# Attention weights loaded as F32 on the SP and ACT queues, mask tiles of twice the size, and deeper loads in the second half

## The reference

```python
x = x + 0.5 * ffn(layernorm(x))          # hidden 4096, inner 11008, int8 weights with scales
x = x + attn(layernorm(x))
x = x + 0.5 * ffn(layernorm(x))

def attn(data, mask, weight, bias):      # weight, mask: 4096 x 4096; mask is int32
    bm = mask.reshape(128, 32, 128, 32).sum(axis=(1, 3)) > 0
    wb = weight.reshape(128, 32, 128, 32) * bm[:, None, :, None]
    return einsum('bsk,nk->bsn', data, wb.reshape(4096, 4096)) + bias

def ffn(x, ...):
    hidden = silu(qlinear(x, w_gate, s_gate)) * qlinear(x, w_up, s_up)
    return qlinear(hidden, w_down, s_down)
```

## Time and profile before

| what | us |
|---|---|
| median of the 2 runs shown | 9921.1 (9498.07 and 10344.14) |
| the profiled execution, whole | 8834.6 |
| its span on the slowest core (core 4) | 8832.8 |
| spans of all cores in it | 8821.7 to 8832.8 |
| mean granted TensorE clock of its cores | 0.944 to 0.963 |

### The profile page before, as it was taken

How to read it: one execution, slowest core, us unless ns; L and a number is a source line. 1 busy time by engine, 2 the same in 40 slices (tenths; PEclk the granted TensorE clock), 3 DMA queues, 4 the chain that set the end, 5 groups by cost and what they waited for, 6 DMA issues and landing times.

```text
span 8832.8 us, 84484 instructions; the slowest of 8 cores (8821.7 to 8832.8 us)
## 1 busy us (share of the span) xinstructions
PE 8020.2 (91%) x35567; PEld 3595.1 (41%) x36280; DVE 1532.0 (17%) x2276; ACT 1263.1 (14%) x1500; POOL 635.9 (7%) x1204
## 2 busy tenths in 40 slices
PE   5399999999577999999975999999997899999998
PEld 1144444444223444444442444444433344444444
DVE  0211111111443111111112111111112211111111
ACT  0511010012121101101014100101132210010111
POOL 1000000000000000000000000000000000000000
PEclk9599999999788999999986999999998999999998
DMA  9133434444484444443431444444333344444343
GB/s 158 57 143 145 155 153 148 152 153 141 105 174 133 153 151 153 162 144 153 150 133 70 153 150 152 152 151 158 148 121 100 127 153 147 153 153 154 148 151 134
DMA packets 201976, 1256.71 MB, mean 142 GB/s; under 512 B 23169, under 2 KB 23298, under 8 KB 113410
## 3 DMA queue, kind: packets, MB, share of 16 engines
q0 software_dynamic: 172800, 1149.32, 38.1%
q10 hardware_dynamic: 18432, 67.12, 2.1%
q1 hardware_dynamic: 10370, 34.83, 1.3%
HBM read 726.88 MB, written 50.33 MB: 88 GB/s over the span
## 4 chain that ended last, share of the span: by engine, by line
PE 88%; DVE 4%; DMA 3%; ACT 3%; issue 2%; DVEq 0%; ACTq 0%; SPq 0%; POOL 0%; POOLq 0%
PE PB L580 27%; PE PB L495 27%; PE PB L501 27%; PE PB L692 4%; DMA MB16D<-mask 2%; DVE WTM L651 1%; DVE XN L440 1%; ACT L341 1%; DMA wtmc<-WTM 1%; PE PB L278 1%; PE PB L737 1%; DVE GS L433 1%; DVE XN L436 1%; ACT L761 0%; ACT L303 0%
## 5 line engine op out<-in xcount | busy, mean ns | idle before, releaser
L495 PE MATMUL PB<-XN,GBUF 128*128 128x512 bf16 x10784 | 2425.6, 380 | 97.3 <-DVE XN L440 85.7
L501 PE MATMUL PB<-XN,UBUF 128*128 128x512 bf16 x10788 | 2417.8, 379 | 11.6
L580 PE MATMUL PB<-H,DBUF 128*128 128x512 bf16 x10786 | 2384.5, 380 | 35.6 <-DVE H L539 23.7
L495 PEld LDWEIGHTS PB<-XN,GBUF 128*128 128x128 bf16 x11008 | 1078.9, 98 | 1394.7 <-issue 102.1
L580 PEld LDWEIGHTS PB<-H,DBUF 128*128 128x128 bf16 x11008 | 1073.6, 98 | 1343.3 <-issue 66.0
L501 PEld LDWEIGHTS PB<-XN,UBUF 128*128 128x128 bf16 x11008 | 1077.0, 98 | 1298.9
L525 ACT ACT_TABLE_LOAD x344 | 441.4, 1283 | 5808.0 <-DVE GS L517 5808.0
L692 PE MATMUL PB<-XN,WTM 128*128 128x512 bf16 x2006 | 500.4, 409 | 215.2 <-DVE WTM L651 152.7
L592 DVE SCALAR_TENSOR_TENSOR R<-PB,SDV,R 128x512 f32<-128x512 f32 x384 | 288.3, 751 | 2148.6 <-PE PB L580 2098.3
L532 DVE SCALAR_TENSOR_TENSOR US<-PB,SUV,RB 128x512 f32<-128x512 f32 x344 | 258.5, 752 | 2092.7 <-PE PB L501 2092.7
L517 DVE SCALAR_TENSOR_TENSOR GS<-PB,SGV,RB 128x512 f32<-128x512 f32 x344 | 258.3, 751 | 1866.5 <-PE PB L495 1866.5
(11 more groups left out here) (58 smaller groups left out, 1205.1 us busy)
## 6 DMA issues: line engine op xcount, KB each, us to landing
GBUF<-wg POOLq DMA_DIRECT2D x344, 1024.0 KB, 5.1
UBUF<-wu POOLq DMA_DIRECT2D x344, 1024.0 KB, 7.1
DBUF<-wd POOLq DMA_DIRECT2D x256, 928.0 KB, 4.7
DBUF<-wd POOLq DMA_DIRECT2D x128, 896.0 KB, 4.7
ABUF<-wa POOLq DMA_DIRECT2D x64, 512.0 KB, 9.0
wtmc<-WTM ACTq DMA_DIRECT2D x64, 512.0 KB, 6.4
XIN<-x SPq DMA_DIRECT2D x32, 512.0 KB, 3.7
out<-OUT ACTq DMA_DIRECT2D x32, 512.0 KB, 2.6
```

The source lines that it names most:

```text
L495: ins = t.matmul(PB[0 + 2 * par][:], GB[par][:, dk * 128:(dk + 1) * 128], XN[:, dk * TH:(dk + 1) * TH], start=(dk == 0), stop=(dk == NDK - 1))
L501: ins = t.matmul(PB[1 + 2 * par][:], UB[par][:, dk * 128:(dk + 1) * 128], XN[:, dk * TH:(dk + 1) * TH], start=(dk == 0), stop=(dk == NDK - 1))
L580: ins = t.matmul(PB[4 + bpar][:], DB[spar][:, ik * 128:(ik + 1) * 128], H[:, ik * TH:(ik + 1) * TH], start=(ik == 0), stop=(ik == nik - 1))
```

## The change

Three edits. (1) The mask is loaded in 32 pieces of 128 x 4096 instead of 64 of 128 x 2048; the four buffers grow to 8 KB a partition, and INDR moves to the place of BMEP. (2) In the first half's attention wa is loaded as F32, without a cast, into two buffers instead of three, by SP for even slots and by ACT for odd slots instead of by POOL; the load of slot sl waits for mask sl-2 instead of sl-3, and the first two wait for the end of gate and up only. (3) In the second half the loads of wtmc run four slots ahead instead of two, each of the four WTM buffers with a semaphore of its own.

```diff
-    MB16A = sb("MB16A", [128, 2048], BF16, 161504)
-    MB16B = sb("MB16B", [128, 2048], BF16, 165600)
-    MB16C = sb("MB16C", [128, 2048], BF16, 169696)
-    MB16D = sb("MB16D", [128, 2048], BF16, 173792)
-    INDR = sb("INDR", [128, 32 * 128], BF16, 177888)
+    MB16A = sb("MB16A", [128, 4096], BF16, 161504)
+    MB16B = sb("MB16B", [128, 4096], BF16, 169696)
+    MB16C = sb("MB16C", [128, 4096], BF16, 177888)
+    MB16D = sb("MB16D", [128, 4096], BF16, 186080)
+    INDR = sb("INDR", [128, 32 * 128], BF16, 144608)
-    ABUF0 = sb("ABUF0", [128, 16 * 128], BF16, 161504)
-    ABUF1 = sb("ABUF1", [128, 16 * 128], BF16, 165600)
-    ABUF2 = sb("ABUF2", [128, 16 * 128], BF16, 169696)
+    ABUF0 = sb("ABUF0", [128, 16 * 128], F32, 161504)
+    ABUF1 = sb("ABUF1", [128, 16 * 128], F32, 169696)
...
-        for rh in range(64):
-            rt, ch = rh // 2, rh % 2
-            par = rh % 4
+        for rt in range(32):
+            par = rt % 4
...
                 psem.inc(gp.dma_start(
-                    MB16[par][:],
-                    mask[rt * 128:(rt + 1) * 128, ch * 2048:(ch + 1) * 2048]), 16)
+                    MB16[par][:], mask[rt * 128:(rt + 1) * 128, :]), 16)
...
-                for c4 in range(4):
-                    c = ch * 4 + c4
+                for c in range(8):
                     ins = t.matmul(PALL[:, c * 512:(c + 1) * 512],
                                    INDR[:, rt * 128:(rt + 1) * 128],
-                                   MB16[par][:, c4 * 512:(c4 + 1) * 512],
+                                   MB16[par][:, c * 512:(c + 1) * 512],
                                    start=(rt == 0), stop=(rt == 31))
...
-                    par = sl % 3
+                    par = sl % 2
                     wp = sl % 4
-                    qsem = (sem_n[0], sem_n[1], sem_n[2])[par] if hf == 0 else \
-                        (sem_d[0] if sl % 2 == 0 else sem_a[1])
-                    qblk = block.gpsimd if hf == 0 else \
-                        (block.sync if sl % 2 == 0 else block.scalar)
+                    qsem = (sem_d[0] if sl % 2 == 0 else sem_a[1]) if hf == 0 else \
+                        (sem_d[0], sem_a[1], sem_d[1], sem_a[0])[sl % 4]
+                    qblk = (block.sync if sl % 2 == 0 else block.scalar) if hf == 0 \
+                        else (block.sync, block.scalar, block.sync,
+                              block.scalar)[sl % 4]
...
-                            if sl < 3:
-                                eng.wait_ge(sem_t.h, mk[("t_d", hf, 1, 93 + par)])
+                            if sl < 2:
+                                eng.wait_ge(sem_t.h, t_gu1)
                             else:
-                                eng.wait_ge(sem_v.h, mk[("v_msk", hf, sl - 3)])
+                                eng.wait_ge(sem_v.h, mk[("v_msk", hf, sl - 2)])
...
-                            if sl < 2:
+                            if sl < 4:
                                 eng.wait_ge(sem_t.h, t_gu1)
                                 eng.wait_ge(sem_c[sl % 2].h, mk[("a_wtm", 0, 62 + sl % 2)])
                             else:
-                                eng.wait_ge(sem_t.h, mk[("t_am", hf, sl - 2)])
+                                eng.wait_ge(sem_t.h, mk[("t_am", hf, sl - 4)])
```

More of the change, by code:

```diff
@@ L115, in build_nc @@
     MB16 = [MB16A, MB16B, MB16C, MB16D]
-    AB = [ABUF0, ABUF1, ABUF2]
+    AB = [ABUF0, ABUF1]
     WTM = [WTM0, WTM1, WTM2, WTM3]
@@ L153, in build_nc, with pdma, pmm @@
         psems = (sem_g[0], sem_g[1], sem_n[0], sem_n[1])
-        for rh in range(64):
-            rt, ch = rh // 2, rh % 2
-            par = rh % 4
+        for rt in range(32):
+            par = rt % 4
             psem = psems[par]
-            def pdma(gp, rh=rh, rt=rt, ch=ch, par=par, psem=psem):
-                if rh < 4:
+            def pdma(gp, rt=rt, par=par, psem=psem):
+                if rt < 4:
                     gp.wait_ge(sem_d[0].h, d_init)
                 else:
-                    gp.wait_ge(sem_t.h, tmark_prep[rh - 4])
+                    gp.wait_ge(sem_t.h, tmark_prep[rt - 4])
                 psem.inc(gp.dma_start(
-                    MB16[par][:],
-                    mask[rt * 128:(rt + 1) * 128, ch * 2048:(ch + 1) * 2048]), 16)
+                    MB16[par][:], mask[rt * 128:(rt + 1) * 128, :]), 16)
             block.gpsimd(pdma)
             dneed = psem.n
-            def pmm(t, rh=rh, rt=rt, ch=ch, par=par, dneed=dneed, psem=psem):
+            def pmm(t, rt=rt, par=par, dneed=dneed, psem=psem):
                 t.wait_ge(psem.h, dneed)
                 ins = None
-                for c4 in range(4):
-                    c = ch * 4 + c4
+                for c in range(8):
                     ins = t.matmul(PALL[:, c * 512:(c + 1) * 512],
                                    INDR[:, rt * 128:(rt + 1) * 128],
-                                   MB16[par][:, c4 * 512:(c4 + 1) * 512],
+                                   MB16[par][:, c * 512:(c + 1) * 512],
                                    start=(rt == 0), stop=(rt == 31))
                 sem_t.inc(ins)
-                tmark_prep[rh] = sem_t.n
+                tmark_prep[rt] = sem_t.n
             block.tensor(pmm)
```

## The result

The changed kernel is slower by 3.5%: against the runs of the kernel before in the same comparison the ratio is 1.0349, 95% interval 1.0323 to 1.0375. The median of its 11 runs is 9597.62 us (9119.97 to 10674.91), that of ten runs of before 9331.72 us (8830.55 to 10344.14). So taken, the changed kernel takes 9120 to 9154 us and before 8829 to 8837. Spans of single cores go from 9090 to 9160 us with the change, the middle one 9113, and from 8816 to 8834 before, the middle one 8824 or 8825 in each of the three later comparisons.

What follows compares the result with a forecast made beforehand. Feed-forward TensorE lines led the chain; the mask stage ran at its transfers' pace and no engine was full in the first attention. 8834.6 + 304 (odd loads) + 2 (F32 masks) - 5 (second attention) = 9136 us, range 8965 to 9250.

Steps and rivals of the forecast that it cites:

- L: First attention: landing time of the odd wa load, forecast 9.5 us with colliding transfers, from 5.3 alone to 11.1.
- Order of ACT's stream: First attention: the odd load stands behind the even slot's write-back on ACT, so cannot leave before the even mask is done.
- The 16 matmuls B: First attention: TensorE's second 16 matmuls of a block, forecast 5.5 us, between 3.5 and 6.8.
- Block: First attention: one output block takes 21.7 us against 12.2, times 32 giving +304 us.
- Even loads and two buffers at no cost: First attention: even loads on SP with two buffers instead of three stay hidden, no cost.
- F32 source: First attention's mask multiplications: F32 instead of bf16 source adds 8 ns each, +2 us in all.
- Mask stage: Mask loads, 32 of 2 MB instead of 64 of 1 MB: same bytes, 0 us, with bounds of -11 and +1.9 us.
- Second attention: Second half: wtmc loads four slots ahead remove TensorE's waits, -5 us, with 0 and -6 as bounds.
- No collision: Rival, first attention: odd load waits its turn but is served as if alone, L 5.3; 9001 us, chance 0.18.
- Heavier collision: Rival, first attention: eight cores read and write at once and the PE stays slow; 9232 us, chance 0.11.
- The load gets past the wait: Rival, first attention: odd loads leave a block ahead, block stays at 12.2 us; 8832 us, chance 0.06.
- Mask stage bound per packet: Rival, mask stage: half the packets take half of 206 us, -103 us, total 9033; chance 0.03.

Runs made afterwards that it cites:

- the loads' change alone: Kernel before with edit (2) only: F32 loads, two buffers, SP and ACT, in the changed kernel's order; 9143.34 us, 1.035.
- the attempt to better the kernel: Kernel before with the next block's loads, masks and write-backs put ahead of L705, in both halves, bf16 cast by POOL; 8940.23 us, 1.2% more than before.
- the cast version: Kernel before with the next block's masks ahead of the residual in the first half only, bf16 cast by POOL; 8768.0 and 8772.6 us, ratio 0.9931.

## Why the prediction was right or wrong

**What it missed.** The stated time, 9136 us, and its range, 8965 to 9250, do not hold the median of the runs, 9597.62. The term of the sum that failed is its base, 8834.6 us: "I forecast on the profiled execution's footing". The median of the kernel before in the same comparison is 9331.72 us, 497 us above that base, and on this base the same sum, +304 + 2 - 5, gives 9633 us, 35 us from the measured median. The two runs shown stood 7.5% and 17% above the profiled execution and the prediction said so, yet its range ended at 9250, below the lower of them, 9498. Nothing in the change or the rows could tell how many of the runs would lie near the profile; with two runs shown, both far above it, either a range that reached up to them (9136 x 9921 / 8835 = 10259) or a ratio was called for.

**What it got.** The mechanism was right. On its own footing the sum was 3.4%, and 3.5% was measured by the slowest cores, 3.3% by the middle ones. That it comes so near is in part luck: L differs by 2 us from core to core, 64 us over 32 blocks, and 9.5 happens to lie inside. Its steps, with core 2 of the profile after:

- *Order of ACT's stream:* right, and shown twice, by moving the load ahead (loss gone) and by adding the lateness alone to the kernel before (about three quarters of it, by four cores).
- *Issue of the odd load:* 2.96 us after the masks begin; measured 3.05 (2707.67 to 2710.72).
- *Landing L:* 9.5 forecast. DVE goes on 9.41 us after the issue in the block shown; the median over the stage is 10.1 us on core 2, 10.6 on core 3, and 8.6 on cores 4 to 6. That L differs by 2 us between cores of one execution was not foreseen. It makes most of the 60 us between the spans of core 4 and core 2: DVE waits 302.2 us for the loads on core 4 and 343.0 on core 2, 41 us more, and 180.7 and 197.7 us for the matmuls ahead of L702, 17 us more.
- *Second mask to TensorE:* 2.85 forecast, 2.65 measured.
- *The 16 matmuls B:* 5.5 forecast; 6.49 in the block shown (2722.78 to 2729.27), 5.14 in the one before it (2701.62 to 2706.76). Over the 32 blocks DVE waits 197.7 us for TensorE ahead of L702, 6.18 a block, of which 0.39 lies outside these matmuls in the block shown (6.88 - 6.49): B is 5.8 us on average, and by the same working 5.3 on core 4. The forecast, a mean of two blocks, lies between.
- *Block:* 21.7 forecast, 22.5 measured on core 2 (721 us / 32); of the difference 0.7 us is L and 0.3 B. Stage: +304 forecast, +330 on core 2. The whole came 318 us above the profile of before on that core, and 258 on core 4.
- *Even loads and two buffers at no cost:* right for the buffers (8839 us with two). No wait for the even load is seen, but it makes 4 of the 10.1 us of the odd load's landing on core 2; holding it back brought about 80 us. The prediction had this collision as part of L.
- *F32 source:* +2 us forecast, L648 takes 684 ns against 685: nothing. The double rate on 16-bit data of the Trainium skill, VectorE: DVE Perf Modes (The perf-mode tier table), was rightly not charged: 685 ns with bf16 is no double rate beside 684 with F32.
- *Mask stage:* 0 forecast; 0 within the spread of 7 us between profiles. The bound of -11 us compared a load whose written bytes alone are larger (GBUF, int8 read and bf16 written) with one of x, while this edit doubles the bytes read as well. The Trainium skill, DMA: Bandwidth & Descriptors (Bandwidth), advises at least 1 MiB a transfer; the larger pieces brought nothing here, where the old ones already read 1 MB each, four in flight, at a share of 1.03.
- *Second attention:* -5 forecast with -6 as a bound; it is -8 (301.6 to 293.8 us), so the bound, the 5.8 us of waits, was too tight.

**The rivals.** *No collision* (9001 us) is refuted by the landing, 10.1 us against 6.1 when the even load is held back. *Heavier collision* is near on core 3 (L 10.6), but B, 5.8 us on average on core 2, is not 6.8. *The load gets past the wait* is refuted: the odd load leaves 3.05 us into the block. *Mask stage bound per packet* is refuted by the equal GB/s (163 and 166) with half the packets (9208 and 4608).

What stays open is why loads land up to 2 us later on some cores. The place on the chip does not decide it. The cores go in pairs, 0 with 1, 2 with 3, and so on, and the pair that is late changes: in the profile after, cores 2 and 3 are slowest (9150.5 and 9150.3 us, L 10.1 and 10.6); in the execution that took 9147.20 us they are among the fastest (9099.2 and 9092.0), and cores 0 and 1 are the slowest (9142.5 and 9145.6); in the profile of the loads' change alone cores 4 and 5 have an L of 9.8 us and the six others 8.6 to 8.8. With the even load held back no pair is late (6.0 and 6.1 us), so it is a part of the collision. Why two cores go together was not tested.

## What to carry to other kernels

Before a load is moved to another engine's queue, write down that engine's stream around it and read which wait stands directly ahead: its own condition says when it may leave, the wait in front says when it does. A prefetch counts from there. The same holds for whatever stands behind a load that waits: in the attempt to better the kernel it was the cast that another engine needed. Where two loads are released by one event, the one that is needed first should be issued first, or the other held back. And where the runs shown lie far from the profiled execution, forecast a ratio, and let the range of the time reach the runs as well as the profile.

## What the runs showed of the hardware

- Holding a transfer back made the kernel faster: 1 MB F32 loads landed in 6.1 us with the other load held back and in 8.6 to 10.6 when it left with them; the whole gained about 80 us.
- Loads that collided landed later by pairs of cores: 9.8 us on two cores and 8.6 to 8.8 on the six others in one profile, 10.1 and 10.6 on another pair in a second profile. Without the collision all eight had 6.0 or 6.1.
- A cast from F32 to bf16 in the transfer costs next to no time against a plain F32 load of the same source bytes: 10.6 and 10.3 us to landing, 317 and 313 us for the same masks, at a DMA share of 0.98 and 0.94. The GB/s that the profile shows, 207 with the cast and 313 without, don't tell the rate: they count a cast load as the 512 KB that it writes. Counted with the 1 MB that it reads, the cast version moves about 309 (an estimate: 2 x 30.94 + 30.92 MB in 300 us).
- The granted clock of TensorE in the first attention went with its pauses: 0.91 to 0.95 where it need not wait for the masks, 0.85 with 3 us a block, 0.71 on core 2 of the changed kernel with 7 and 3 us a block.
